# A GNN and MoE megakernel on one core: sums moved ahead of the third ternary piece, transposes moved inside products, and six pieces quantised in the linear layer's last tiles

## The reference

```python
edge_index = jnp.stack([src, dst])
x = x + _L0_gnn_ref(_layernorm(x), edge_weight, L0_gnn_bias, edge_index)   # W[src, dst] += weight; x @ W.T + bias
x = x + _L0_ffn_ref(_layernorm(x)[None], wg, w1, b1, w2, b2)[0]            # 8 experts, top 2, capacity 314, relu
x = x + _L1_gnn_ref(_layernorm(x), edge_index, W, b)                       # h = x @ W.T + b; out[row] += norm * h[col]
x = x + _L1_ffn_ref(_layernorm(x)[None], w1, w2)[0]                        # int8-like activations, ternary weights, gelu
```

## Time and profile before

| | us |
|---|---|
| median of 3 runs | 1117.19 |
| lowest and highest run | 1112.7 and 1119.63 |
| profiled execution, its own time | 1121.93 |
| its span | 1120.2 |
| PE busy in the span | 991.2 (88%) |
| DVE busy | 751.6 (67%) |
| ACT busy | 459.1 (41%) |
| POOL busy | 161.7 (14%) |
| mean granted TensorE clock | 0.948 of full |

### The profile page before, as it was taken

One profiled execution on the slowest core, in us unless ns is written; L12 is line 12 of the kernel. 1 busy time (PEld: TensorE's weight loads), 2 busy tenths in 40 slices (PEclk: granted clock), 3 DMA queues, 4 the chain that ended last, 5 costly groups with the idle time before them and its releaser, 6 DMA issues.

```text
span 1120.2 us, 17433 instructions
## 1 busy us (share of the span) xinstructions
PE 991.2 (88%) x6750; PEld 544.8 (49%) x6750; DVE 751.6 (67%) x1040; ACT 459.1 (41%) x558; POOL 161.7 (14%) x218
## 2 busy tenths in 40 slices
PE   0799789995899999999489998788879999999997
PEld 0688545442655555555234443333434444444443
DVE  7998778888566666658685834877777555555540
ACT  3388536552244444444321124776724211111121
POOL 6200053331310000100432100222110000000000
PEclk9898889998699999999799999998989999999999
DMA  4657425545667777763587655677610444545440
GB/s 138 203 200 259 147 76 188 214 181 199 214 210 254 251 256 253 253 247 126 174 152 193 160 169 188 206 243 239 213 38 20 113 114 112 112 112 112 113 94 34
DMA packets 170193, 189.95 MB, mean 170 GB/s; under 512 B 130666, under 2 KB 130988, under 8 KB 166032
## 3 DMA queue, kind: packets, MB, share of 16 engines
q1 hardware_dynamic: 163727, 166.52, 47.9%
q0 software_dynamic: 6400, 22.55, 6.4%
HBM read 137.98 MB, written 35.86 MB: 155 GB/s over the span
## 4 chain that ended last, share of the span: by engine, by line
PE 66%; DVE 19%; issue 5%; DMA 5%; ACT 2%; POOL 1%; DVEq 0%; SPq 0%; ACTq 0%; POOLq 0%
PE ps L1260 13%; PE ps L1289 12%; PE ps L1052 11%; PE ps L1160 8%; PE ps L1245 6%; PE ps L1176 5%; DVE stats L1705 3%; DVE fq L2202 2%; PE ps L1117 2%; DMA eo_d<-eo 2%; DVE xl L1868 2%; PE ps L1221 1%; DVE w1l L2040 1%; DMA xt<-xt_d 1%; PE ps L947 1%
## 5 line engine op out<-in xcount | busy, mean ns | idle before, releaser
L1260 PE MATMUL ps<-w1q,xqt 128*128 128x512 fp8e4 x640 | 142.0, 383 | 4.9 <-DVE x L2256 4.9
L1289 PE MATMUL ps<-w2q,hqt 128*128 128x512 fp8e4 x640 | 140.8, 379 | 1.4 <-DVE out_t L2314 1.4
L1586 ACT ACTIVATE hf<-ps,fs 128x512 f32<-128x512 f32 x80 | 55.0, 687 | 183.7 <-PE ps L1260 183.5
L2295 DVE TENSOR_REDUCE hm<-hf 128x1 f32<-128x512 f32 x80 | 54.3, 685 | 79.0 <-ACT hf L1586 78.9
L1260 PEld LDWEIGHTS ps<-w1q,xqt 128*128 128x128 f16 x640 | 63.0, 99 | 81.7 <-issue 8.1
L1289 PEld LDWEIGHTS ps<-w2q,hqt 128*128 128x128 f16 x640 | 62.3, 98 | 75.9 <-DVE out_t L2314 1.9
L1052 PE MATMUL ps<-gwt_h,xt 128*128 128x512 f16 x320 | 85.6, 389 | 7.3 <-DMA xt<-xt_d 5.8
L1052 PE MATMUL ps<-wt_h,xt 128*128 128x512 f16 x320 | 86.7, 383 | 0.8 <-issue 0.8
L1160 PE MATMUL ps<-xdh,w1h 128*128 128x314 f16 x256 | 76.9, 301 | 3.5 <-DVE w1l L2040 2.7
L1160 PE MATMUL ps<-xdh,w1l 128*128 128x314 f16 x256 | 76.3, 298 | 0.0
L1160 PE MATMUL ps<-xdl,w1h 128*128 128x314 f16 x256 | 76.2, 298 | 0.0
(11 more groups left out here) (316 smaller groups left out, 1989.8 us busy)
## 6 DMA issues: line engine op xcount, KB each, us to landing
abs_in<-in_L_ffn_w SPq DMA_DIRECT2D x32, 1024.0 KB, 6.8
wstage<-in_L_ffn_w SPq DMA_DIRECT2D x32, 1024.0 KB, 8.3
fnat_b<-in_L_ffn_w SPq DMA_DIRECT2D x28, 512.0 KB, 4.8
fnat_a<-in_L_ffn_w SPq DMA_DIRECT2D x27, 512.0 KB, 4.7
eo_d<-eo SPq DMA_DIRECT2D x16, 512.0 KB, 2.9
hq_d<-hq SPq DMA_DIRECT2D x8, 1024.0 KB, 6.3
xs_d<-xs_all SPq DMA_DIRECT2D x10, 512.0 KB, 3.0
bias_b<-in_L_ffn_w SPq DMA_DIRECT2D x9, 512.0 KB, 5.6
```

The lines of the kernel that those rows point to most:

```text
L1260: last = mm(ps[:, n % 4, :], xqt[:, u, k, :], w1q[:, k // 2, n * 512:(n + 1) * 512, k % 2], start=(k == 0), stop=(k == KD - 1))
L1289: last = mm(ps[:, 4 + h, :], hqt[:, u, k, :], w2q[:, k // 2, h * 512:(h + 1) * 512, k % 2], start=(k == 0), stop=(k == KF - 1))
L1586: cp(hf[:, i % 2, n * 512:(n + 1) * 512], ps[:, n % 4, :], ACT.Gelu, scale=fs[:, i % 2, 3:4]).then_inc(s_ge, 1)
L2295: last = v.tensor_reduce(hm[:, u, n:n + 1], hf[:, u, n * 512:(n + 1) * 512], AX.X, ALU.max, apply_absolute_value=True)
```

## The change

- LayerNorm scalars: DVE's copy of the sums becomes an addition of the row (0, 1e-5) (`no_eps`), so that POOL's `rstd_tile` is one power in place of an addition, a power and a multiplication. The factor 1024 (`SX`) that the multiplication gave moves into `high` (an ACT scale) and into `low` and `y_low` (a scalar_tensor_tensor in place of a tensor_tensor).
- First products: PE's transposes of tile n+1 stand ahead of block k = 3 inside product n for every tile, where before this held for the first product and the others had them ahead of product n. POOL adds the bias of tile i+2 as soon as tile i's result is in x, ahead of its two `rstd_tile`; before it waited for `y_norm(i)` of the next round.
- Linear layer: `FIRST` is 3. The third tile (n = 12) is turned by PE, ahead of block k = 3 of product 11, and its two stores and its transposing load go.
- Ternary pieces: DVE quantises 0 and 1 in the linear layer's tile 8 and 2 to 5 in its tile 9; PE turns 0 and 1 ahead of blocks k = 2 and k = 5 of product 18, and 2 and 3 at the same places of product 19. ACT takes four signs ahead of `h_high(8)` and two ahead of `h_high(9)`; it copies the banks only after the linear layer, where the signs of 6 and 7 stand first. SP loads pieces 7 to 10 ahead of piece 6.
- Aggregation: tile i takes pieces 4+6i to 9+6i. Tile 0 turns 4, 5 and 6 after blocks 4 to 6, 7 ahead of block 9, and 8 and 9 after its end. `agg(i-1)` comes after the second piece of tile i on DVE.
- Last layer: PE waits for the last aggregation tile's `agg` ahead of its third group of columns, not of the first.

```diff
@@ -129,6 +129,7 @@
         bias_b = sb("misc", "bias_b", [P, D], F32)
...
         mv_one = sb("misc", "mv_one", [P, 2], F32)
+        no_eps = sb("misc", "no_eps", [P, 2], F32)
         mv = sb("misc", "mv", [P, NT, 2], F32)
@@ -469,7 +468,7 @@
...
-        FIRST = 2
+        FIRST = 3
@@ -507,7 +506,7 @@
...
-            return range(7 * i, min(7 * i + 7, 64))
+            return range(4 + 6 * i, 10 + 6 * i)
@@ -694,7 +693,7 @@
             for i in range(NT):
...
                     rows_turned(R_LIN1 + i + 1)
-                if i + 2 < NT:
+                if i + 2 < NT and by_transfer(R_LIN1 + i + 2):
                     rows_out(R_LIN1 + i + 2)
@@ -705,12 +704,17 @@
             sp.wait_ge(s_mix, 2 * NT)
...
                 ternary_rows(n)
+
+            def next_rows(n):
+                sp.wait_ge(s_fq, 4 + n - NF + 1)
+                ternary_rows(n)
+
+            for n in range(NF, NF + 4):
+                next_rows(n)
             sp.wait_ge(s_mmread, 2 + R_LIN1 + NT)
-            for n in range(NF - 1, 64):
-
-                if n >= NF:
-                    sp.wait_ge(s_fq, 4 + n - NF + 1)
-                ternary_rows(n)
+            ternary_rows(NF - 1)
+            for n in range(NF + 4, 64):
+                next_rows(n)
@@ -769,6 +773,8 @@
         def _(pool):
...
             ok = dict(allow_small_or_imprecise_dtypes=True)
+            g.memset(no_eps[:, 0:1], 0.0)
+            g.memset(no_eps[:, 1:2], LN_EPS)
             g.iota(thr[:, :], [[WIN, NTH]], base=0, channel_multiplier=0, **ok).then_inc(s_iota, 1)
@@ -803,17 +809,13 @@
             g.affine_select(out=tri[:, :], in_=ones16[:, :], pattern=[[1, P]], compare_op=ALU.is_ge,
...
-            def rstd_tile(n, i, k, mv=mv, rstd=rstd):
+            def rstd_tile(n, i, mv=mv, rstd=rstd):
...
                 pool.wait_ge(s_stat, n + 1)
-                g.tensor_tensor(rtmp[:, 0:1], mv[:, one, 1], consts[:, 0:1], ALU.add).then_inc(s_pl, 1)
-                pool.wait_ge(s_pl, 2 * n + 1)
-                g.tensor_tensor(rtmp[:, 1:2], rtmp[:, 0:1], consts[:, 1:2], ALU.pow).then_inc(s_pl, 1)
-                pool.wait_ge(s_pl, 2 * n + 2)
-                g.tensor_tensor(rstd[:, one], rtmp[:, 1:2], consts[:, k:k + 1], ALU.mult).then_inc(s_rstd, 1)
-
-            rstd_tile(0, 0, 2, mv0, rstd0)
+                g.tensor_tensor(rstd[:, one], mv[:, one, 1], consts[:, 1:2], ALU.pow).then_inc(s_rstd, 1)
+
+            rstd_tile(0, 0, mv0, rstd0)
@@ -837,12 +839,12 @@
             biased(1)
...
             for i in range(NT):
-                rstd_tile(3 + 2 * i if i < 7 else 10 + i, i, 2)
+                if 0 < i < NT - 2:
+                    pool.wait_ge(s_mmread, 2 + R_GNN0 + i + 1)
+                    biased(i + 2)
+                rstd_tile(3 + 2 * i if i < 7 else 10 + i, i)
                 if i + 3 < NT:
-                    rstd_tile(4 + 2 * i, i + 3, 2, mv0, rstd0)
-                if 0 < i < NT - 2:
-                    pool.wait_ge(s_yn, i + 1)
-                    biased(i + 2)
+                    rstd_tile(4 + 2 * i, i + 3, mv0, rstd0)
                 if i == 0:
@@ -1037,14 +1039,26 @@
                     pe.wait_ge(s_xth, turned(n) + 1)
...
+            def weight_piece(n):
+
+
+                pe.wait_ge(s_fq, 4 + n + 1)
+                pe.wait_ge(s_fc, n + 1)
+                packed = fq[:, n % 2, :].bitcast(F16)
+                for k in range(KD // 2):
+                    last = tr(bank16(4 + n % 4)[:, k * P:(k + 1) * P], packed[:, k * P:(k + 1) * P], id16[:, :])
+                last.then_inc(s_ft, 1)
+
             def product(n, u, rh, rl):
...
                 for k in range(KD):
-                    if k == 3 and n in (R_GNN0, R_LIN1):
+                    if k == 3 and n not in (R_LIN1 - 1, R_LIN1 + NT - 1) and not by_transfer(n + 1):
                         transposes(n + 1, 1 - u)
+                    if k in (2, 5) and n >= R_LIN1 + NT - 2:
+                        weight_piece(2 * (n - R_LIN1 - NT + 2) + k // 5)
                     if k == KD - 1 and n < R_LIN1:
@@ -1057,8 +1071,6 @@
...
                 for i in range(NT):
-                    if 0 < i < NT - 1 and not by_transfer(r + i + 1):
-                        transposes(r + i + 1, 1 - i % 2)
                     body(i, i % 2)
@@ -1244,10 +1246,11 @@
                         for h in range(2):
...
                                       start=False, stop=(b == NT - 1 and a == 1))
-                    if todo and b >= 3 and (i > 0 or b < NT - 1):
+                    if todo and (b >= 3 if i > 0 else 4 <= b < 7):
                         weight_piece(todo.pop(0))
-                assert not todo
                 last.then_inc(s_agg, 1)
+                for n in todo:
+                    weight_piece(n)
@@ -1255,6 +1258,8 @@
                 for n in range(8):
...
                     pe.wait_ge(s_ge, 8 * i + n + 1)
+                    if isinstance(i, int) and i == 0 and n == 2:
+                        pe.wait_ge(s_aggread, 2 + NT)
                     hold(pe)
@@ -1293,7 +1298,7 @@
...
-            pe.wait_ge(s_aggread, 2 + NT)
+            pe.wait_ge(s_aggread, 2 + NT - 1)
             ffn_in(0, 0)
@@ -1403,11 +1408,11 @@
...
                 act.wait_ge(s_xn, n + 1)
-                cp(parts(n, u)[0], xn[:, slot(n, u), :], ACT.Copy).then_inc(s_xh, 1)
+                cp(parts(n, u)[0], xn[:, slot(n, u), :], ACT.Copy, scale=SX).then_inc(s_xh, 1)
...
                 act.wait_ge(s_yn, i + 1)
-                cp(xs_all[:, i, 0:D], xn[:, 0, :], ACT.Copy).then_inc(s_yh, 1)
+                cp(xs_all[:, i, 0:D], xn[:, 0, :], ACT.Copy, scale=SX).then_inc(s_yh, 1)
@@ -1430,15 +1435,17 @@
                     high(r + 1, 1)
...
                     u = i % 2
-                    if 0 < i < NT - 1 and not by_transfer(r + i + 1):
-
-                        act.wait_ge(s_mm, r + i + 1)
+                    turn = i < NT - 1 and not by_transfer(r + i + 1)
+                    if turn and (r == R_GNN0 or i == 0):
+                        if i > 0:
+                            act.wait_ge(s_mm, r + i + 1)
                         copy_high(r + i + 1, 1 - u)
-                    if i == 0:
-                        copy_high(r + 1, 1)
                     if i + 2 < NT:
...
                         high(r + i + 2, u)
+                    if turn and r == R_LIN1 and i > 0:
+                        act.wait_ge(s_mm, r + i + 1)
+                        copy_high(r + i + 1, 1 - u)
                     body(i, u)
@@ -1531,9 +1538,12 @@
...
+                if i == NT - 2:
+                    act.wait_ge(s_swh, 1)
+                    for n in range(4):
+                        upper_sign(n)
                 if i == NT - 1:
-                    act.wait_ge(s_swh, 1)
-                    for n in range(2):
+                    for n in range(4, 6):
                         upper_sign(n)
@@ -1557,9 +1567,11 @@
             normalised(R_LIN1, h_high)
...
+            for n in range(6, 8):
+                upper_sign(n)
             act.wait_ge(s_mm, 1 + R_LIN1 + NT)
             for n in range(64):
-                if n + 2 < 64:
+                if 8 <= n + 2 < 64:
                     upper_sign(n + 2)
@@ -1707,9 +1719,10 @@
                 hold(dve)
...
                 dve.wait_ge(s_bn, 3 * n + 3)
-                v.tensor_copy(mv[:, i, :], mv_one[:, :]).then_inc(s_stat, 1)
+                v.tensor_tensor(mv[:, i, :], mv_one[:, :], no_eps[:, :], ALU.add).then_inc(s_stat, 1)
             dve.wait_ge(s_x0, 16)
+            dve.wait_ge(s_iota, 1)
             statistics(0, 0, mv0)
@@ -1865,7 +1879,8 @@
             def low(n, u):
...
                 hi, lo = parts(n, u)
-                v.tensor_tensor(lo, xn[:, slot(n, u), :], hi, ALU.subtract).then_inc(s_xl, 1)
+                v.scalar_tensor_tensor(out=lo, in0=xn[:, slot(n, u), :], scalar=SX, in1=hi, op0=ALU.mult,
+                                       op1=ALU.subtract).then_inc(s_xl, 1)
@@ -1874,7 +1889,8 @@
...
                 dve.wait_ge(s_yh, i + 1)
-                v.tensor_tensor(xs_all[:, i, D:2 * D], xn[:, 0, :], xs_all[:, i, 0:D], ALU.subtract).then_inc(s_yl, 1)
+                v.scalar_tensor_tensor(out=xs_all[:, i, D:2 * D], in0=xn[:, 0, :], scalar=SX, in1=xs_all[:, i, 0:D], op0=ALU.mult,
+                                       op1=ALU.subtract).then_inc(s_yl, 1)
@@ -1960,7 +1976,6 @@
                 elif i == NT - 2:
...
                     do(v.reciprocal(std0[:, :], rstd0[:, :]))
-                    do(v.tensor_scalar(std0[:, :], std0[:, :], SX, None, ALU.mult))
                 if i == 0:
@@ -2227,22 +2242,24 @@
                     mixed(i + 3, 0)
...
                     low(R_LIN1 + i + 2, u)
+                if 0 < i < NT - 1 and not by_transfer(R_LIN1 + i + 1):
+                    dve.wait_ge(s_mm, R_LIN1 + i + 1)
+                    copy_low(R_LIN1 + i + 1, 1 - u)
                 if i + 3 < NT:
...
-                if i == NT - 1:
-                    weight_piece(0)
```

(13 more changed lines are left out.)

28 lines of the change are left out of this document (10 added, 18 removed).

## The result

The changed kernel takes 1105.76 us (median of 20 runs, 1100.46 to 1115.43), the kernel before 1114.3 (20 runs, 1111.12 to 1126.15). The ratio is 0.992, 95% interval 0.9894 to 0.9946: a gain of 8.5 us where I forecast 24. The profiled execution took 1104.58 us, 17.3 under that of before. The two differences don't agree, and this is about half of the answer: some 7 us of the 24 are missing between the two profiles, and some 9 more because the profiled execution of before was a long one.

A forecast was written before the change was run, and what follows sets the result against it. PE, busiest at 88%, was taken as kept waiting in four places. Terms -3.0 -0.2 -0.3 -7.6 +6.5 -19.7 = -24.3 took the profiled 1121.93 to 1097.6 us; less 4.7, 1093 (own range 1088 to 1098, outer 1082 to 1107).

The forecast's parts named there:

- First products, -3.0: First products: PE needs `low` later, POOL's addition no longer meets it, PE sets the pace; 3.0 us saved.
- Rival 4: First products: bn_stats is held by POOL's bias addition; 3 us lost, 1096 us; chance 0.05.
- the shorter `rstd_tile`: First products: saves 0.4 us at each DVE wait for it, off PE's path in this stage.
- Third linear tile, -7.6: Linear layer: the 5.81 us load wait and 2.7 of slow clock go, transposes cost 0.9; 7.6 us saved.
- Rival 1: Linear layer: the load wait moves to the fourth tile, 3.4 us plus up to 2.7; 1099 us; chance 0.17.
- 6 to 8 us of landing: Linear layer: the fourth tile's transposing load takes 6 to 8 us and lands ahead of need.
- Pieces in products 18 and 19, +6.5: Last two linear products: two 2.45 us waits (4.9), four turns (0.9), clock dips (0.7); 6.5 us lost.
- Aggregation, -19.7: Aggregation: tile 0 at 22.8 us, plain tiles at 11.75; tile 0 to piece 63 falls from 147.5 to 127.8 us.
- Gating and ahead of the linear layer, -0.5: Gating: one operation less, -0.2 us; ahead of the linear layer: shorter `rstd_tile` once on the path, -0.3 us.
- Last layer, 0: Last layer: the 10.43 us from piece 63 to its start stay, despite the weaker wait; 0 us.
- Rivals 2, 3 and 5: Aggregation: 12.9 us tiles, 1103 (0.14); PE alone sets tiles, 1085 (0.10); many waits leave PE at 1.2 GHz, 1140 (0.04).
- Rival 6: Linear products and aggregation: turned pieces hold PE longer, tile 0 eats the saving; some 15 us lost, 1108; chance 0.05.

The follow-up runs named there:

- no_meet: Changed kernel with POOL's first bias additions held until DVE's first two `low` are done: 1096.73 us, ratio 0.9843 to the kernel before.
- rstd_held: p_rstd with POOL's first bias additions held until DVE's first two `low` are done: 1113.87 us, ratio 0.9972 to the kernel before.
- p_rstd: Kernel before with only the shorter `rstd_tile`, the bias additions ahead of it and the moved factor `SX`: 1115.2 us, ratio 1.0009.
- only_third: Kernel before with the third linear piece turned by PE and no other transposes moved: 1110.76 us, ratio 0.9928.
- third_moved: Changed kernel with the third linear piece turned by the transposing load again (`FIRST = 2`): 1100.64 us, ratio 0.9897 to the kernel before.
- third_moved2: third_moved run once more, beside the changed kernel on the same chip: 1106.03 us, ratio 0.9895 to the kernel before.
- after: Changed kernel, first measurement and profile: median 1105.76 us, ratio 0.992 to the kernel before; profiled execution 1104.58 us.
- after_third: Changed kernel, no edit, run beside third_moved2 on the same chip: 1107.03 us, ratio 0.9895 to the kernel before.
- after_again: Changed kernel once more, no edit: 1106.72 us, ratio 0.9904 to the kernel before.
- later_turns: Changed kernel with pieces in the last two linear products turned at the fifth and eighth step: 1098.44 us, ratio 0.9866 to the kernel before.
- three one-edit kernels: Changed kernel with one edit each: no_meet 1096.73 us, later_turns 1098.44 us, and ACT's four bank copies ahead of signs 6 and 7, 1097.61 us.
- no_pieces: Changed kernel without the schedule of the ternary pieces: 1113.1 us, ratio 0.9995 to the kernel before.
- p_pieces: Kernel before with only the new schedule of the ternary pieces: 1107.05 us, ratio 0.9925.

## Why the prediction was right and wrong

The mechanisms of the two large terms were right: the late load and the waits for ternary pieces were there, and the edits removed them. The sum failed in four steps: the start, the third linear tile, the pieces in products 18 and 19, and the aggregation of before. In means of three profiles each (before 1114.9, after 1105.8 us of span, a difference of 9.1 that agrees with the medians' 8.5) the stages differ by +6.0 start, -2.6 products, -1.2 middle, +5.4 linear, -16.8 aggregation, +0.1 last layer. Of the +6.0, 3.55 is the kernel's, the rest is the launches'. The +5.4 of the linear layer, where I forecast -7.6 + 6.5 = -1.1, is the largest miss: -5.2 for the load that is gone, +1.9 for the late seventh load of one launch, +7.8 for the pieces, +0.9 for a lower clock in the first product.

- **First products, -3.0**: right. From the first result to the tenth it is -3.0 in every profile, for the reason given (PE sets the pace); the -2.6 of the stage has the first product in it, whose clock differs between launches. The small addition was blocked as foreseen. What I didn't see is that the transposes alone would have given the same. Rival 4 is refuted: bn_stats, two in 1.29 us beside POOL's addition, wasn't held. In this the Trainium skill, SBUF — State Buffer, "SBUF: two separate sides", agrees with the rows: an operation of DVE with one input from SBUF, outside the two-port modes, is free of the lock, and the addition with two inputs is not (0.63 us for 0.16).
- **The step that failed and that no launch excuses stands in that same part: the shorter `rstd_tile` "saves 0.4 us at each wait of DVE", off PE's path.** I followed what the faster engine gives to DVE and not what it does next itself. POOL is done with two rstd in 1.74 us and starts bias additions 0.8 us ahead of DVE's `low` instead of 1.2 behind it, so the collision removed from the tiles of the first products (six of ten had a `low` of 3.06 us) is made anew in front of the first. The term stood at nothing; its price is 3.55 us in every profile. no_meet and rstd_held remove it. It takes the whole of the part's gain (p_rstd: 1.0009).
- **Third linear tile, -7.6**: mis-sized by its source. In the profiled run the term is exact: from the first linear result to the third it took 28.5 us, and 20.85 after. But the wait of 5.81 and the 2.7 us of low clock stood in that one run; six further profiles of kernels with that load waited 0.56 (at the next piece), 5.20, 3.01, 1.81, 1.99 and 0.18 (at the next piece), and rstd_held 0. Alone in the kernel before it is worth 6 us in the median (only_third); in the changed kernel nothing (third_moved and third_moved2 against the changed kernel). In means of three profiles of each kernel the load's removal is worth 5.2 us. Rival 1, that the wait moves on to a later load, was at 0.17; it happened in one of the three profiles of the changed kernel, at the seventh tile and not the fourth. The argument for 6 to 8 us of landing was right: the first load left took 6.2 us in all three. Why the removed load took 8.0 us in one launch and 12.1 in another was not settled.
- **Pieces in products 18 and 19, +6.5**: the waits are 2.51 and 2.50 where I had 2.45, in every profile. The low clock behind them is what I undersized: the last two products take 6.2 us more than without pieces in `after`, 7.7 in after_third and 9.5 in after_again. So the term is 7.8 in the mean, not 6.5; the count without a dip, 5.8, and with both, 8.6, had the right shape. What the forecast took as given, that the pieces stand at the third and sixth step, was the costly choice: later_turns pays 1.1 us for the same work.
- **Aggregation, -19.7**: mis-sized by 3 us (-16.8), on the side of before. In the changed kernel my hand count holds: tiles 11.9 for 11.75, tile 0 22.6 us for 22.8 (its waits 2.64 for 3.1 and 1.46 for 1.8), and from tile 0 to the turn of piece 63 it is 803.54 - 675.0 = 128.5 for 127.8. But the kernel before took 157.7 us in the profiled run, and 154.7, 155.1 and (with this stage unchanged) 155.4 to 157.3 in others: the 15.7 us tiles of the earlier trace rows, where the plain one takes 14.36, come in every profile of this stage, but two of them, three, or four (the profiled run) among tiles 2 to 8.
- **The median**: I set the forecast 4.7 below the profile's own scale by three runs (1117.19). Over 11 to 31 runs the kernel before has medians of 1114.3 to 1116.9, so the profiled run, 1121.93, was 5 to 7.6 us too long, and taking 4.7 off the level did not take anything off the gain. Its span is 5.3 us above the mean of the three profiles of before: 2.0 in the linear layer and 1.9 in the aggregation, which two of my terms removed, and 1.8 in the start, which none did. A gain taken from one long run was counted as if every run had it.
- **Gating and ahead of the linear layer, -0.5**: the first is within what the middle stage varies (290 to 294), not shown. For the second, from the first transposes to the first linear product it takes 3.51 or 3.52 us in the twelve profiles with the new rstd and 4.03 in the six with the old: 0.5 for 0.3. **Last layer, 0**: right.
- Rivals 2, 3 and 5 didn't occur: tiles of 11.9 at clock 1.00. Rival 6, "less than it says", had the time about right (1108) and its mechanism half: the pieces in the products did pay more than reckoned, the rest of the loss lies at the start and in the loads. That 1105.76 lies inside my outer range (1082 to 1107) is luck: its upper end stood there for tiles of 12.9 us, which didn't occur.

Open: how much of the good medians of the three one-edit kernels is the earlier first rstd, why no_pieces kept so little of its parts, and what makes the clock ahead of the first rstd differ between launches.

## What to carry to other kernels

When an edit makes an engine faster, follow that engine to its own next instruction and ask whom it now meets; here POOL's gain of 0.4 us an operation cost 3.55 us on the critical path. A wait for a transfer in one profile is a draw, not a size: look at the same stage in several executions before subtracting it, and check how far the profiled run stands above the median. Where PE takes in side work, place it where its operand is already there: two steps later in the product saved 5 to 8 us in the linear layer, and no wait came back elsewhere.

## What the runs showed of the hardware

- POOL's and DVE's two-input operations exclude each other for their whole length, in turn: two `low` and two bias additions that meet take 6.27 and 5.99 us, apart 2.36 and 4.64. From the start of the first to the end of the last they take 7.1 us, which is the sum of the lengths apart (7.0). A tiny one waits too: the 128x2 addition took 0.63 us beside POOL's addition and 0.16 when free.
- A wait of 2.51 us on PE left the granted clock at 1.00 in one profile (after, 648 to 660 us) and came with 0.86 in another (p_pieces), with the same products ahead of it. Of 16 such waits 5 had the lower clock, which made the product 1.4 to 1.7 us longer.
- A transposing load, issued at the same point of the program, took 8.0 to 12.1 us to land in eight launches and ended with PE waiting from 0 to 5.81 us; in some launches the late one is the fourth or the seventh instead.
- The same work at the start of a launch was done 7 us sooner or later (135.9 to 142.9), with PE's granted clock from 80 to 135 us between 0.97 and 0.82.
